# Column groups that hold tokens, turned by VectorE, whole first rows, and two sums on GpSimd, in a layer on one Trainium2 core

## Reference

```python
xn = layernorm(x)                                  # over the last axis
s = attn(xn)      # g = sigmoid(u @ gate_w.T + gate_b); u_mean = mean_t(u*g); d_eff = d + u_mean @ d_lr_u @ d_lr_v / 4
                  # G = cumprod(tanh(a)); y = c * G * cumsum(b*u*g / G) + d_eff * u*g
g = silu(ffn(xn)) # probs = softmax(xr @ wr.T), 8 routes; top 2 of them, normalised gates
                  # h = silu(xr @ w1.T); h = silu(h @ w3.T); h = h @ w2.T
                  # out[indices_k] += gates_k * h      (rows 0..7 of the output only)
x = x + s * g
```

## Time and profile before

| | |
|---|---|
| median of 3 runs | 757.16 us |
| profiled execution, its own time | 758.42 us |
| its span, first to last instruction | 756.6 us |
| mean granted TensorE clock | 0.998 |
| PE busy | 747.4 us, 99%, 3565 instructions |
| weight loads (PEld) | 598.6 us, 79% |
| VectorE (DVE) | 507.9 us, 67%, 480 instructions |
| ScalarE (ACT) | 342.6 us, 45% |
| GpSimd (POOL) | 45.6 us, 6%, 55 instructions |
| chain that ended last | PE 83%, DVE 7%, ACT 5% |

### The profile page before, as it was taken

How to read it: one execution, slowest core, us unless ns; L and a number is a source line. 1 busy time by engine, 2 the same in 40 slices (tenths; PEclk the granted TensorE clock), 3 DMA queues, 4 the chain that set the end, 5 groups by cost and what they waited for, 6 DMA issues and landing times.

```text
span 756.6 us, 8790 instructions
## 1 busy us (share of the span) xinstructions
PE 747.4 (99%) x3565; PEld 598.6 (79%) x3565; DVE 507.9 (67%) x480; ACT 342.6 (45%) x440; POOL 45.6 (6%) x55
## 2 busy tenths in 40 slices
PE   8999999999999999999999999999999999999997
PEld 7878877887788787888788878878788778877875
DVE  6889888775867495479989996574534562456321
ACT  5869784745682335242944373235122431324122
POOL 3302203020302000000000000000000000000000
PEclk9999999999999999999999999999999999999999
DMA  9744863546352543566596704240232223010500
GB/s 342 280 167 167 281 222 123 209 147 225 143 182 78 186 153 111 223 209 245 171 382 194 298 29 162 88 165 29 112 139 83 112 87 129 35 56 1 223 1 3
DMA packets 27977, 117.21 MB, mean 155 GB/s; under 512 B 3808, under 2 KB 4000, under 8 KB 20896
## 3 DMA queue, kind: packets, MB, share of 16 engines
q1 hardware_dynamic: 18688, 99.85, 36.5%
q10 hardware_dynamic: 9248, 16.80, 5.9%
HBM read 95.60 MB, written 37.77 MB: 176 GB/s over the span
## 4 chain that ended last, share of the span: by engine, by line
PE 83%; DVE 7%; ACT 5%; issue 3%; POOL 1%; DMA 1%; SPq 0%; DVEq 0%; POOLq 0%; ACTq 0%
PE main L1019 26%; PE main L1020 26%; PE main L1021 26%; PE lgp L1086 1%; PE spare L1103 1%; PE lgp L1103 1%; ACT rows L881 1%; DMA wh6f<-x 1%; DVE x1f L1155 1%; DVE wl3f L1155 1%; DVE wl5f L1155 1%; DVE x3r L1155 1%; ACT rows L883 1%; DVE x8f L1155 0%; PE main L1138 0%
## 5 line engine op out<-in xcount | busy, mean ns | idle before, releaser
L1155 DVE TENSOR_TENSOR s<-s,main 128x512 f32<-128x512 f32 x72 | 48.5, 683 | 59.5 <-PE main L1021 59.4
L1155 DVE TENSOR_TENSOR u<-u,main 128x512 f32<-128x512 f32 x36 | 24.5, 684 | 42.0 <-PE main L1021 42.0
L953 ACT ACTIVATE u<-u 128x512 f32<-128x512 f32 x32 | 20.0, 631 | 57.7 <-DVE u L1155 57.7
L934 ACT ACTIVATE s<-main 128x512 f32<-128x512 f32 x36 | 20.8, 596 | 54.4 <-PE main L1021 28.5
L1155 DVE TENSOR_TENSOR u<-s,main 128x512 f32<-128x512 f32 x32 | 21.7, 684 | 32.9 <-PE main L1021 32.9
L953 ACT ACTIVATE rows<-rows 128x512 f32<-128x512 f32 x16 | 10.1, 632 | 71.3 <-DVE rows L1155 71.3
L953 ACT ACTIVATE s<-s 128x512 f32<-128x512 f32 x32 | 20.0, 630 | 47.9 <-DVE s L1155 47.8
L1155 DVE TENSOR_TENSOR rows<-s,main 128x512 f32<-128x512 f32 x16 | 11.0, 687 | 30.4 <-PE main L1021 30.4
L953 ACT ACTIVATE u<-main 128x512 f32<-128x512 f32 x32 | 18.7, 590 | 20.4 <-PE main L1021 20.4
L883 ACT ACTIVATE rows<-rows,nm 128x1024 f32<-128x1024 f32 x23 | 26.5, 1153 | 0.8
L881 ACT ACTIVATE rows<-rows 128x1024 f32<-128x1024 f32 x24 | 25.2, 1051 | 0.0
(11 more groups left out here) (702 smaller groups left out, 2433.0 us busy)
## 6 DMA issues: line engine op xcount, KB each, us to landing
out<-x SPq DMA_DIRECT2D x31, 512.0 KB, 7.7
rows<-x SPq DMA_DIRECT2D x26, 512.0 KB, 4.3
H_d<-u ACTq DMA_DIRECT2D x32, 256.0 KB, 3.9
H_d<-s ACTq DMA_DIRECT2D x16, 256.0 KB, 2.9
rows<-xh_d SPq DMA_DIRECT2D x16, 256.0 KB, 5.6
w2f<-w2T SPq DMA_DIRECT2D x2, 2048.0 KB, 10.3
wl6f<-wB SPq DMA_DIRECT2D x3, 1024.0 KB, 8.2
wl4f<-wB SPq DMA_DIRECT2D x3, 1024.0 KB, 6.5
```

What stands on the lines that cost most here:

```text
L934: eng.activation(s1[:, j, :], bk, ACT.Copy).then_inc(s_pa, 1)
L953: ins = eng.activation(dst, src, ACT.Silu)
L1155: return eng.tensor_tensor(o, a, b, op)
```

## The change

- Logits: each of the four column groups now holds tokens. For every tile of 128 tokens, group q takes tokens 32q to 32q+31; all four k-blocks are added up in PSUM. `LQ` has 16 matmuls of 128 columns instead of 4 of 512, and fills 128 columns of the bank instead of 512. `PH` is built in the same way. `RT` then turns blocks of 32x32 with VectorE's transpose, from PSUM into SBUF, and copies the eight routes. `LE` and `RA` are gone.
- End: `FA`, `sel` and `FT`'s matmuls are gone; `FT` is one VectorE transpose of 128x128 from PSUM each. `y` is padded to 32 columns, turned by VectorE at the end of `AT2`, and brought into place by 16 small DMAs (`Y8`, on SP's queue behind `W2`).
- Start: rows 0 and 1 are loaded whole, one DMA each; both statistics wait for the whole row.
- `T 1` and `S 4` of unit 0 are done by GpSimd, at their places in the list, with a semaphore of their own, `s_gp`. `S 4` waits for `S 2`, `T 1` for `T 2` and the first `LQ`.

```diff
@@ plan()
-            at(0, 2, 3, "LE", 0)
-            at(0, 3, 2, "RA", 0)
-            at(0, 3, 2, "LE", 1)
-            at(0, 4, 1, "RA", 1)
-                at(n, *((0, 2) if first else (-1, 3)), "LE", c)
-                at(n, *((1, 0) if first else (0, 2)), "RA", c)
-                at(n, 1, 3, "LE", c + 1)
-                at(n, *((3, 0) if first else (2, 0)), "RA", c + 1)
-    at(NN - 1, 6, 2, "FA", 0)
+    at(NN - 1, 3, 2, "Y8", 0)
-    steps.append(("FA", 1))
-    steps.append(("Y8", 0))
     steps.append(("FT", 1))
-    steps.append(("Y8", 1))
...
+        yt = lg[:, 0:KT * Q].rearrange("p (k e) -> p k e", e=Q)
+        def in_group(v, q):
+            return v.rearrange("p (j q i) -> p q j i", q=NQ, i=Q)[:, q, :, :]
...
@@ sync
-                    c0 = 0
-                    if r < 2:
-                        c0 = HT
-                        eng.dma_start(row_buf(r)[:, 0:HT], x01[r, 0]).then_inc(s_rh[r], 16)
-                    src = x01[r, 1] if r < 2 else x[r * P:(r + 1) * P, :]
-                    eng.dma_start(row_buf(r)[:, c0:D], src).then_inc(s_row[r if r < 8 else 4 + r % 2], 16)
+                    eng.dma_start(row_buf(r), x[r * P:(r + 1) * P, :]).then_inc(s_row[r if r < 8 else 4 + r % 2], 16)
+                elif kind == "Y8":
+                    wait(s_oz, 1)
+                    wait(s_yt, 1)
+                    for q in range(NQ):
+                        for g in range(NQ):
+                            eng.dma_start(y8[rows8[q], :].rearrange("e (k c) -> e k c", c=P)[:, :, Q * g:Q * (g + 1)],
+                                          yt[rows8[g], 2 * q:2 * q + 2, :]).then_inc(s_ye, 16)
...
@@ gpsimd
+                elif s == ("T", 0, 1):
+                    raw_in(wait, 0, "a")
+                    raw_in(wait, 0, "b")
+                    wait(s_xs[0], 16)
+                    t_in(wait, 0, 2)
+                    wait(s_lq, nth("LQ", 0, "a"))
+                    a = xf(0, "a")
+                    eng.tensor_tensor(a, xf(0, "b"), a, ALU.subtract).then_inc(s_gp, 1)
+                elif s == ("S", 0, 4):
+                    wait(s_wl[6], wloads[(0, 6)])
+                    s_in(wait, 0, 2)
+                    wait(s_wh, nth("WH", 0, 1))
+                    wait(s_wo, nth("WO", 0, 1))
+                    eng.tensor_tensor(w_f(6, 1), w_f(6, 1), w_from(0, 2), ALU.subtract).then_inc(s_gp, 1)
...
@@ tensor
-                    for q in range(NQ):
-                        ins = eng.matmul(lgp[h][Q * q:Q * (q + 1), :], wr32[:, NQ * kh + q, :], xf(n, b)[:, q, :],
-                                        start=(kh == 0), stop=(kh == 1))
+                    for k in range(4):
+                        for q in range(NQ):
+                            ins = eng.matmul(lgp[h][Q * q:Q * (q + 1), 0:P].rearrange("p (j i) -> p j i", i=Q),
+                                             wr32[:, 4 * kh + k, :], in_group(xf(n, b)[:, k, :], q),
+                                             start=(kh == 0 and k == 0), stop=(kh == 1 and k == 3))
-                elif kind == "RA":
...
-                        ins = eng.matmul(acc[o][Q * j:Q * (j + 1), :], Pz[:, 8 * u + 4 * h + j, :], c_buf(n, i, j),
-                                        start=(u == 0 and h == 0), stop=(u == NU - 1 and h == 1))
+                        for q in range(NQ):
+                            ins = eng.matmul(acc[o][Q * q:Q * (q + 1), 0:P].rearrange("p (k i) -> p k i", i=Q),
+                                             Pz[:, 8 * u + 4 * h + j, :], in_group(c_buf(n, i, j), q),
+                                             start=(u == 0 and h == 0 and j == 0), stop=(u == NU - 1 and h == 1 and j == 3))
...
@@ vector
-                elif kind == "T":
+                elif kind == "T" and s != ("T", 0, 1):
...
-                elif kind == "S":
+                elif kind == "S" and s != ("S", 0, 4):
...
-                    wait(s_ra, c + 1)
-                    quarters = lgp[c % 2][:, :].rearrange("p (j q e) -> p j e q", q=NQ, e=Q)[:, :, 0:E, :]
-                    eng.tensor_reduce(L[:, 4 * c:4 * c + 4, :], quarters, AX.X, ALU.add).then_inc(s_rt, 1)
+                    wait(s_lq, 2 * (c + 1))
+                    wait(s_rt, c)
+                    turned = lg[:, 0:P]
+                    link(eng.transpose(turned, lgp[c % 2][:, 0:P]))
+                    eng.tensor_copy(L[:, 4 * c:4 * c + 4, :], turned.rearrange("p (j e) -> p j e", e=Q)[:, :, 0:E]).then_inc(s_rt, 1)
...
+                elif kind == "FT":
+                    i = s[1]
+                    wait(s_ph, nth("PH", NN - 1, 6 if i else 5))
+                    wait(s_oz, 1)
+                    k0 = 4 * (1 - i)
+                    eng.transpose(o32[:, k0:k0 + 4, :].rearrange("p k e -> p (k e)"), acc[1 - i][:, 0:P]).then_inc(s_ft, 1)
```

More of the change, by code:

```diff
@@ L359, in places_of, with program @@
     raise ValueError("no place for the last rows")
-def program(nc, x, x01, xT, wB, w11, w2T, small, out):
+def program(nc, x, xT, wB, w11, w2T, small, out):
     steps = plan()
@@ L607, in vacated @@
             if was == ("T", 0, 4):
-                wait(s_t, nth(*was))
+                t_in(wait, 0, 4)
                 wait(s_hi, nth("HI", 0, 2))
@@ L611, in vacated @@
             elif was == ("T", 0, 1):
-                wait(s_t, nth(*was))
+                t_in(wait, 0, 1)
                 wait(s_lq, nth("LQ", 0, "b"))
@@ L640, in s_in, with t_in, count_of @@
         def s_in(wait, w, k):
-            wait(s_s, nth("S", w, k))
+            if (w, k) == (0, 4):
+                wait(s_gp, 2)
+            else:
+                wait(s_s, count_of("S", w, k))
+        def t_in(wait, n, k):
+            if (n, k) == (0, 1):
+                wait(s_gp, 1)
+            else:
+                wait(s_t, count_of("T", n, k))
+        def count_of(kind, *a):
+            return nth(kind, *a) - (nth(kind, 0, 1 if kind == "T" else 4) < nth(kind, *a))
         def w_in(wait, w, i):
@@ L706, in program @@
         ending = [bank[(NN - 1, 6, j)] for j in range(4)]
-        FB = [b for b in range(BANKS) if b not in ending] + ending[:1]
+        FB = [b for b in range(BANKS) if b not in ending][0]
         fb_user = {}
@@ L873, in link @@
                 wait(s_ac, count[0])
-            wait(s_po, 3)
+            wait(s_po, 2)
             eng.activation(nm[:, :], mhalf[:, 0:1], ACT.Silu)
@@ L1110, in _ @@
                     eng.matmul(lgp[0][:, 0:RANK], ones, prs[:, :], start=True, stop=True).then_inc(s_at, 1)
-                elif kind == "Y8":
-                    i = s[1]
-                    wait(s_y, 1)
-                    if i:
-                        wait(s_ye, i)
-                    for q in range(4):
-                        ins = eng.matmul(lgp[0][rows8[2 * i + q // 2], (q % 2) * P:(q % 2 + 1) * P], y[:, 4 * i + q, :],
-                                        ident[:, :], start=True, stop=True)
-                    ins.then_inc(s_yt, 1)
-                elif kind == "FT":
-                    i = s[1]
-                    if i:
-                        wait(s_fc, 1)
-                    else:
-                        wait(s_fv, 1)
-                        wait(s_pv, pv(*fb_user[FB[0]]))
-                    for k in range(4 * (1 - i), 4 * (1 - i) + 4):
-                        ins = eng.matmul(main[FB[0]][:, k * E:(k + 1) * E], lg[:, (k % 4) * P:(k % 4 + 1) * P], sel[:, :],
-                                         start=True, stop=True)
-                    ins.then_inc(s_ft, 1)
                 elif kind == "FM":
@@ L1188, in _ @@
                     t = s[1]
+                    row_loaded(wait, t)
                     src = row_buf(t)
                     st = bst[:, nth(*s) % 2, :]
[L1191 to L1194 removed]
                     eng.bn_stats(st[:, 0:6], src[:, 0:HT])
[L1196 removed]
                     link(eng.bn_stats(st[:, 6:12], src[:, HT:D]))
@@ L1209, in _ @@
                     wait(s_mv, k)
-                    wait(s_po, 4 + NQ)
+                    wait(s_po, 3)
                     if k > 1:
@@ L1272, in _ @@
                         raw_in(wait, n, "b")
-                        if n:
-                            wait(s_hi, nth("HI", n, 0))
-                            wait(s_lo, nth("LO", n, 0))
-                        else:
-                            wait(s_xs[0], 16)
-                            wait(s_t, nth("T", 0, 2))
+                        wait(s_hi, nth("HI", n, 0))
+                        wait(s_lo, nth("LO", n, 0))
                         if n < GATE:
@@ L1289, in _ @@
                         raw_in(wait, n, "d")
-                        wait(s_t, nth("T", n, 1))
+                        t_in(wait, n, 1)
                         ins = tt(xf(n, "f"), d, a, ALU.subtract)
@@ L1299, in _ @@
                         raw_in(wait, n, "c")
-                        wait(s_t, nth("T", n, 2))
+                        t_in(wait, n, 2)
                         if n:
@@ L1464, in _ @@
                     wait(s_fe, 1)
-                    wait(s_ye, 2)
```

(1 more changed line is left out.)

87 lines of the change are left out of this document (19 added, 68 removed).

## The result

The changed kernel takes 760.65 us (median of 6 runs, 759.85 to 761.08) against 757.14 us for the kernel before (6 runs, 756.16 to 757.57): a ratio of 1.0047, 95% interval 1.0034 to 1.006. It is slower, by 3.5 us. The profiled execution took 759.87 us, its span is 758.0 us.

What follows compares the result with a forecast made beforehand. TensorE, busy 99% of the span, was taken as the bound. Gains of 6.4 us against losses of 9.6 put 3.2 us on the median 757.16: 760.4 us; own range 757.5 to 763, range asked for 749.8 to 763.8.

Steps and rivals of the forecast that it cites:

- The hold: Unit 0: GpSimd's T 1 and S 4 each keep VectorE's two-SBUF-input instructions (S 2, WO 2) waiting 4.3 us.
- rival A: Unit 0: GpSimd's long read doesn't hold VectorE up; only gains remain, 750.8 us; chance 0.24.
- rival B: Unit 0: VectorE gets in again after the first hold, WO 2 before S 4; 755.0 us; chance 0.12.
- Rival C: Unit 0: VectorE always goes first, GpSimd reads only in its idle time, WO 4 late; 758.4 us; chance 0.08.
- not for the whole of GpSimd's: VectorE against GpSimd: VectorE needn't wait for the whole of a GpSimd instruction; the path is free once its reading is over.
- TensorE's stall: Before tile (0, 2), due at 57.24 us: TensorE starts it at about 65.1, 7.9 us lost.
- The clock: Behind the idle time before tile (0, 2): TensorE at half speed, costing 1.0 to 2.2 us, taken as 2.0.
- Column groups: LQ and PH, 32 groups of 16 matmuls over 128 columns: 0.86 to 0.9 us each, nothing gained or lost.
- rival D: LQ and PH: the column groups pay per instruction, 6 to 28 us on top, 767 to 788 us; chance 0.10.
- Tail: From the last PH to FM: one transpose from PSUM lets FM start at about 749.1, 1.65 us gained.
- Start: Rows 0 and 1 loaded whole: row 1 lands at about 6.4 us, 0.3 us gained.
- The wait near 102 us: TensorE's 0.8 us wait on a producer stays, since its chain starts again from a PE result at 88.66.

Runs made afterwards that it cites:

- experiment 4: Changed kernel with T 1 and S 4 of unit 0 still on GpSimd, but only after VectorE has finished WO 2: 755.56 us, ratio 0.9975.
- experiment 3: Changed kernel with S 4 of unit 0 alone back on VectorE, behind WO 2; T 1 stays on GpSimd: 756.31 us, ratio 0.9986.
- Experiment 6: Changed kernel with 64 unused TensorE transposes filling the wait ahead of tile (0, 2): 759.82 us, ratio 1.003.
- experiment 7: Changed kernel with T 1 and S 4 of unit 0 back on VectorE and rows 0 and 1 loaded in halves again: 751.91 us, ratio 0.9931.
- experiment 2: Kernel before with only T 1 and S 4 of unit 0 moved to GpSimd: 766.4 us, ratio 1.0115.

## Why the prediction was right

The forecast was 760.4 us and 760.65 came. The mechanism is the one named, at its place and in its size. That the total came within 0.3 us is luck in part: gains and loss were both taken too high, by nearly the same amount. Point by point:

- **The hold: right.** The value taken was 4.3, the middle between two ways to count (3.4 and 5.1 us), neither of which gives it; 4.3 came out each of the three times that GpSimd's instruction had just begun (the 2.4 and 3.7 us more of experiment 4 are what was left of it). `WO 2` was forecast to end at 65.0 and ended at 63.62, with everything there 1.4 us earlier. GpSimd got in at the border of two instructions, as the earlier trace rows had let one expect. The sign that was named for it was the wrong one, though: `S 2` was to start near 53.9, and its record starts at 48.31, on time, as rival A wanted it. The hold is read from where it ends, 54.89. Rivals A to C fell by the ends of `S 2` and `WO 2`; nearest to rival B's state comes experiment 3, with `S 4` on VectorE: 755.0 forecast for B, 756.31 measured there, where the clock cost 1.6 us in place of 1.0. (Rival C's sum takes 67.9 for the end of `WO 4` before; the trace has 68.70. Nothing else rests on it.)
- **But "not for the whole of GpSimd's" was wrong.** I read that from a `pow` over one element. That row stands, VectorE's instruction at 33.42 kept its length beside it; it was carried over to 2048 columns, where it doesn't hold. `T 1` ran from 48.28 to 52.74, 4.46 us, and `S 2` got only what came after. The page "SBUF — State Buffer" of the Trainium skill (Who interferes with whom) is right at this size. The figure of its "GPSIMD Engine Reference" (Performance versus the Vector engine), 4497 ns for an addition of 2048 columns, agrees with the 4.46 us of the subtraction here.
- **TensorE's stall: right**, 7.8 us for 7.9. **The clock: right in the trace, not in the time.** The 11 steps from matmul to matmul behind the wait (63.72 to 68.21) take 4.49 us in place of 2.5: 2.0 us as forecast. Experiment 6 shows that 0.9 of them would be waited for anyway, and 0.8 us came out in the time. I had priced the slow stretch without asking whether the next operands were there sooner.
- **RA, FT 0: right.** Eight times 0.446 and once 0.90 us in a trace of before, and nothing of it in the changed one.
- **Column groups: nearly right.** Four `LQ` and the first step to the next tile take 44.88 - 41.24 = 3.64 us against 3.57 before; over all 32 groups I count about 0.5 us lost. The forecast was zero; rival D (6 to 28 us) is false. The rows:

```profile
41.24 1.08 PE L1078 MATMUL lgp<-x0f,cst 128*32 128x128 f32 x32
42.14 1.06 PE L1078 MATMUL lgp<-x1f,cst 128*32 128x128 f32 x32
...
44.88 0.50 PE L1010 MATMUL main<-x2r,wh3r 128*128 128x512 f32 x1
```

- **Tail: right.** From the last `PH` to `FM 1` it is 752.13 - 750.63 = 1.50 us; before, 750.77 - 747.66 = 3.11. That is 1.6 us for 1.65. The rows that answer:

```profile
750.63 1.06 PE L1091 MATMUL lgp<-s,bc 128*32 128x128 f32 x32
...
752.13 1.93 PE L1107 MATMUL main<-w2f,tail 128*32 128x256 f32 x32 [0.44 <-DVE tail L1426]
```

- **Start: 0.3 us forecast; its size stays open.** In the trace of the changed kernel it looks like 1.8 us: `NB 0` starts at 7.31 in place of 8.24, and the clock stays at 1.00. But the 0.8 us of clock belong to the one profiled execution of before, and are the larger part of the 1.26 us by which it lay over its median. Of the rest, experiment 7 finds nothing in the time, while the traces put it between 0.1 and 1.3 us.
- **The wait near 102 us: wrong.** "Stays, for its chain starts again from a PE result" looked at where VectorE's chain begins and not at the other engine that it meets. GpSimd's statistics arrived earlier against it in the late kernel, and 1.3 us were saved from tile to tile. So the loss in the trace is 7.8 + 2.0 - 1.3 = 8.5 us, in place of 9.6.

In the time the gains are 5.0 us in place of 6.4 and the loss 8.5 in place of 9.6: 3.2 forecast, 3.5 measured. Part of both errors lies outside the traces. The time of a run exceeds its span by 1.8 to 2.0 us in the kernel before, by 1.9 to 2.0 in the changed one and by 2.2 to 2.8 in its variant without GpSimd's two instructions; no run shows why. By the medians of the spans (755.4 before, 749.8 without the two, 758.65 changed) the gains are 5.6 us and the loss is 8.9. The 5.6 us are what the terms sum to without a start: 3.6 + 0.9 + 1.6 - 0.5. The loss is 0.4 us over the 8.5 of the trace; the profiled execution lies 0.7 us under its own median span, and the mean granted clock of the six executions goes from 0.993 to 0.996, so how long the clock stays low may differ from one to the next. No trace shows that for this kernel.

## What to carry to other kernels

Moving a two-input elementwise operation from VectorE to GpSimd doesn't unload VectorE: 2.2 us of it less cost 4.3 us of hold each time. Where VectorE was idle it cost nothing; a place where it gained was not found. Look for it in the profile as instructions that are too long, not as gaps: 6.58 in place of 2.29 us, or 2.22 us for four elements. Where two engines meet like that, which of them is half a microsecond ahead decides, and a change elsewhere can move it: 0.44 us ahead in the changed kernel, 0.64 behind in experiment 6. When an engine runs late, price what follows by what would have been waited for anyway, and read a term at the start from more than one execution before you count it.

## What the runs showed of the hardware

GpSimd's subtraction of 128x2048 from SBUF takes 4.6 us alone and shuts VectorE's instructions with two SBUF inputs out for all of it, while one with a PSUM operand (0.68 us) ran beside it. Where both were waiting, they took turns at the borders of instructions. Behind waits of 3.3, 3.6, 7.7 and 7.7 us (experiments 3 and 4, the changed kernel, experiment 2) TensorE's granted clock was 0.5 (1.2 GHz) over 3.4, 3.4, 4.1 and 6.0 us of its work, in the first two only after 1.5 and 1.1 us at 1.00. Behind 1.8, 1.9 and 2.0 us it stayed at 1.00, and behind 2.1 us it fell once.
